# Two heads of a pair in the two partition halves, and their two kinds of score matmul issued in turn

## The chip, the cores and the metric

The kernel runs on one core of a Trainium2 chip. Five engines share the core: TensorE (PE), VectorE (DVE), ScalarE (ACT), GpSimd (POOL) and SyncE (SP), which here only issues DMAs. The metric is the device time of one execution in microseconds. One execution was also taken by the hardware profiler; all times of single instructions come from it.

## The reference

The input x is 16 batches of 256 tokens by 256 features; the context has the same shape. One block of a gated decoder is computed: cross attention with 16 heads of 16 features, then a feed-forward layer whose weights and activations are quantised.

```python
def xattn(Q, K, V):                      # Q = layernorm(x), K = V = ctx
    q = Q @ Wq.T + bq; k = K @ Wk.T + bk; v = V @ Wv.T + bv     # to 16 heads of 16
    attn = softmax(q @ k^T / 4)
    return (attn @ v) @ Wo.T + bo
x = x + tanh(g_xattn[0]) * xattn(layernorm(x), ctx, ctx)
# ffn: x_q = act_qdq(x); up, gate = act_qdq(x_q @ W^T); gate * u16(sigmoid(gate)); act_qdq; @ w_down^T
# act_qdq: 16 bit, one scale for the whole tensor; the weights have 4 bits, one scale for each 32
x = x + tanh(g_ffn[0]) * ffn(layernorm(x))
```

Because each activation scale is a maximum over the whole tensor, the feed-forward part can only begin when the attention of all batches is done.

## The kernel before

`attention` handles 16 batches, each as 8 steps, one for each pair of heads. A step number g runs from -40 to 158; `divmod(g, 8)` gives the batch `it` and the step `j` in it. Every engine runs the same loop over g, and `batch(g, off)` says whether the piece of work with offset off is due; so the order on each engine is written by hand, and semaphores tie the engines together. This is a software pipeline: in step g TensorE computes the scores of batch it+1 and the turned scores of batch it.

Float32 accuracy is had from float16 parts: `qk` holds the high and the low part of q and of k. `stack_q` and `stack_k` (SP, L251 and L261) copy them by DMA into `qst` and `kst`, where the contraction runs over three pieces: high times high, high times low, low times high.

Before the change the two heads of a pair (r = 0, 1) have their rows interleaved in one stack of 96 partitions. `kst` holds both heads; `qst` exists once for each head, with zeros in the rows of the other head, so that one `kst` serves both. Three `memset`s at the start (POOL L769, DVE L647 and L654) write the zeros. Partition 96 holds ones in `kst` and the row maxima in `qst`.

The steps of the attention, with the names that the change and the rows use:

- Scores, L398 (PE): for each of two token tiles tt and each head r, 96 rows x 128 columns of `qst` against 256 columns of `kst`, into `s_ps[tt]`. Four matmuls in a step.
- Row maxima, L670 (DVE): two reductions of 128x512 in a step, one for each `s_ps`. TensorE may write `s_ps[tt]` of the next step when this reduction of the last step is done (`max_done`).
- Turned maxima: TensorE L353 turns the maxima, ACT L518 writes `mrow`, and `load_tops` (SP, L271) copies it into partition 96 of `qst`, in two halves of a batch (TOP0, TOP1), each by two DMAs.
- Turned scores, L414 (PE): for each key tile kt, 97 rows, 512 columns (both heads) into `st_ps[u % 3]`. Two matmuls in a step. ACT L559 takes the exponential of each (`exp_done`).
- Values, L380 (PE): 16 instructions with 32 output columns each, in the steps j = 0, 2, 4, 6.
- Between these, TensorE has one 12-matmul projection (L341) in each odd step: q in j=1, k in j=3, v in j=5, the output in j=7. The turning of xn (L479) is in j=6, the turned maxima in j=0 and j=4.
- DVE has, besides the maxima: y (L680) in j=0, statistics in j=1 and j=3, the low part of q (L641, `ql_done`) in j=2, the low part of k in j=4 with a reciprocal (L706), and one 128x512 operation in each of j=5, 6, 7.

SP issues all DMAs of the attention in one order. From the low part of q on this is: 6 DMAs of `stack_q`, one load of ctx (L242), 3 DMAs of `stack_k` (L265), 2 of TOP0, one of the reciprocals, 4 of `ot`, and the others. The scores of the next batch wait at j = 0 for `stack_loaded`, the turned scores for `top_loaded[0]`; at j = 4 for `top_loaded[1]`.

Of the kernel before, what the change touches and what calls it, by code (L numbers as in the profile page):

```python
# [28 lines left out]
def attention(nc, t, x, ctx, out):  # L29
# [10 lines left out]
    QA = 4  # L40
    ONES = 0x54005400
# [9 lines left out]
    with ExitStack() as es:  # L51
# [42 lines left out]
        kst = sb("kst", [97, 3, PAIRS, S], F16)  # L94
        qst = sb("qst", [97, 3, 2, PAIRS, S], F16)
# [40 lines left out]
        ones_set = sem("ones_set")  # L136
        qst_zeroed = sem("qst_zeroed")
# [94 lines left out]
        def _(sp):  # L232
# [16 lines left out]
            def stack_q(b):  # L249
# [17 lines left out]

            def load_tops(b, hf):
                sp.wait_ge(top_done[hf], b + 1)
                for r in range(2):  # L270
                    sp.dma_start(qst[96:97, b % 3, r, QA * hf:QA * hf + QA, :], mrow[QA * r:QA * r + QA, hf, :]  # L271
                                 ).then_inc(top_loaded[hf], 16)
# [64 lines left out]
        def _(pe):  # L337
# [49 lines left out]
            for g in STEPS:  # L387
                it, j = divmod(g, PAIRS)
                if 0 <= it + 1 < NB:
                    b = it + 1  # L390
                    if j == 0:
                        pe.wait_ge(stack_loaded[b % 2], 144 * (b // 2 + 1))
                    for tt in range(KT):
                        u = UNITS * b + KT * j + tt
                        if u >= 2:
                            pe.wait_ge(max_done, u - 1)
                        for r in range(2):
                            mm = nc.tensor.matmul(s_ps[tt][:, r, :], qst[0:96, b % 3, r, j, tt * P:(tt + 1) * P],  # L398
                                                  kst[0:96, b % 3, j, :], start=True, stop=True)
                        mm.then_inc(s_done, 1)  # L400
                if 0 <= it < NB:
                    b = it
                    if g == 0:
                        pe.wait_ge(ones_set, 1)
                        pe.wait_ge(w_kept, 4)
                    if j == 0:
                        pe.wait_ge(top_loaded[0], 32 * (b + 1))
                    if j == QA:
                        pe.wait_ge(top_loaded[1], 32 * (b + 1))
                    for kt in range(KT):  # L410
                        u = UNITS * b + KT * j + kt
                        if u >= 3:
                            pe.wait_ge(exp_done, u - 2)
                        nc.tensor.matmul(st_ps[u % 3][:], kst[:, b % 3, j, kt * P:(kt + 1) * P],  # L414
                                         qst[:, b % 3, :, j, :], start=True, stop=True).then_inc(st_done, 1)
# [85 lines left out]
        def _(act):  # L501
# [11 lines left out]
            def tops(b, hf):  # L513
                act.wait_ge(top_turned[hf], b + 1)
                if b:
                    act.wait_ge(top_loaded[hf], 32 * b)
# [16 lines left out]
            for g in STEPS:  # L533
# [5 lines left out]
                if (b := batch(g, -14)) is not None:  # L539
                    act.wait_ge(q_done, b + 1)  # L540
                    if b:
                        act.wait_ge(stack_loaded[(b - 1) % 2], 144 * ((b - 1) // 2 + 1))
# [9 lines left out]
                if 0 <= it < NB:  # L552
# [3 lines left out]
                    for kt in range(KT):  # L556
                        u = UNITS * b + KT * j + kt
# [749 lines left out]
```

## Time and profile before

| | us |
|---|---|
| runs of the kernel before | 668.58, 670.52, 671.84 (median 670.52) |
| the profiled execution | 668.55, of which 666.9 from the first to the last instruction |
| TensorE busy | 567.4 |
| VectorE busy | 500.5 |
| ScalarE busy | 436.1 |
| GpSimd busy | 178.9 |
| mean granted TensorE clock | 0.954 |
| row maxima, L670 | 163.4 in 256 instructions |
| exponentials, L559 | 138.9 in 256 |
| scores, L398 | 80.4 in 512 |
| turned scores, L414 | 77.4 in 256 |
| values, L380 | 69.4 in 1024 |

The attention takes up to about 340 us, the rest is the preparation of the feed-forward weights and the feed-forward part. Busy time is the union of an engine's instructions. TensorE's matmuls are pipelined: a row of 0.60 us for 4 matmuls is followed by the next row 0.44 us after its start. For the rate of an engine the distances between starts count, not the lengths.

### The profile page before, as it was taken

Reading aid. Unit: us, or ns where it says so; the run is one execution under the profiler, and the core shown is the slowest. Engines: PE = TensorE matmul, PEld = TensorE weight load, DVE = VectorE, ACT = ScalarE, POOL = GpSimd, SP = SyncE. Lnnn points to the kernel's source line nnn. Section 1 sums busy time; section 2 is a strip of 40 time slices with the busy share of each in tenths; the row PEclk is TensorE's granted clock in tenths of the full one; section 3 lists DMA queues with packets and bytes.
Section 4 is the critical chain, followed back from the end, with each engine's and each line's share of the span. In section 5 each row is a group of like instructions: output and inputs, shape, how many; then the busy total and the mean of one; then the engine's idle time right before and its main releaser. Section 6 shows DMA issues by size and latency. Waiting matters only on the chain. (4 is left out here: it accounts for less than half of the span.)

```text
span 666.9 us, 12176 instructions
## 1 busy us (share of the span) xinstructions
PE 567.4 (85%) x4268; PEld 340.4 (51%) x4268; DVE 500.5 (75%) x772; ACT 436.1 (65%) x609; POOL 178.9 (27%) x193
## 2 busy tenths in 40 slices
PE   0569999999999999999651799999877779949997
PEld 0335666666666666654330344444333334418886
DVE  4498778999999999888864255467999989964441
ACT  2216777778777777876740244549998588859970
POOL 4412235555566565443542000000000000010000
PEclk9979999999999999999885799999999989979999
DMA  6211244544544444552311000000000000011443
GB/s 213 71 47 57 79 121 132 133 136 119 140 111 137 133 124 120 152 150 66 88 55 37 1 0 1 1 0 0 0 0 0 1 0 0 0 63 64 142 141 94
DMA packets 42175, 48.87 MB, mean 73 GB/s; under 512 B 10384, under 2 KB 29456, under 8 KB 42128
## 3 DMA queue, kind: packets, MB, share of 16 engines
q1 hardware_dynamic: 40976, 44.07, 23.1%
q0 software_dynamic: 1152, 4.19, 2.3%
q8 instruction: 27, 0.44, 0.3%
q14 instruction: 20, 0.16, 0.1%
HBM read 24.51 MB, written 8.65 MB: 50 GB/s over the span
## 5 line engine op out<-in xcount | busy, mean ns | idle before, releaser
L670 DVE TENSOR_REDUCE negm<-s_ps 128x2 f32<-128x512 f32 x256 | 163.4, 681 | 32.7 <-PE s_ps L398 32.3
L559 ACT ACTIVATE pt<-st_ps 128x512 f32<-128x512 f32 x256 | 138.9, 596 | 51.7 <-PE st_ps L414 50.7
L937 PE MATMUL pairs<-xq,wut 128*128 x576 | 127.5, 383 | 21.1 <-DVE cmax L1145 12.9
L937 PEld LDWEIGHTS pairs<-xq,wut 128*128 128x128 f16 x576 | 56.7, 99 | 91.9 <-issue 27.7
L398 PE MATMUL s_ps<-kst,qst 96*128 96x256 f16 x512 | 80.4, 275 | 12.8 <-DVE negm L670 7.0
L414 PE MATMUL st_ps<-qst,kst 97*128 97x512 f16 x256 | 77.4, 383 | 3.8 <-ACT pt L559 3.8
L380 PE MATMUL pv_ps<-pt,vt 128*32 128x256 f32 x1024 | 69.4, 389 | 0.7 <-ACT pt L559 0.6
L937 PE MATMUL pairs<-xq,wgt 128*128 (+1 forms) x288 | 64.5, 384 | 0.0
L398 PEld LDWEIGHTS s_ps<-kst,qst 96*128 96x128 f16 x512 | 46.2, 97 | 34.3 <-DVE negm L670 21.1
L1230 POOL PARTITION_ALL_REDUCE vmax<-vmax x4 | 2.3, 582 | 224.2 <-DVE vmax L1118 224.2
L988 PE MATMUL pairs<-wdt,h 128*128 128x256 f16 x384 | 48.4, 277 | 10.0 <-ACT h L1077 10.0
L1134 DVE TENSOR_REDUCE cmax<-gb (+1 forms) x8 | 26.8, 3353 | 36.9 <-ACT gb L1012 36.9
L761 POOL TENSOR_SCALAR xn<-xt,mv,rstd 128x256 f32<-128x256 f32 x30 | 36.5, 1226 | 66.0 <-PE misc L479 65.9
L1012 ACT COPY gb<-pairs 128x1024 f32 (+1 forms) x24 | 24.3, 1012 | 38.5 <-PE pairs L937 38.5
L380 PEld LDWEIGHTS pv_ps<-pt,vt 128*32 128x32 f32 x1024 | 27.0, 110 | 39.0 <-issue 26.3
L988 PEld LDWEIGHTS pairs<-wdt,h 128*128 128x128 f16 x384 | 38.0, 99 | 15.3 <-ACT h L1077 10.5
L937 PEld LDWEIGHTS pairs<-xq,wgt 128*128 128x128 f16 x288 | 28.3, 99 | 33.5 <-issue 1.7
L504 ACT ACTIVATE qk<-misc,bqk_s 128x256 f16<-128x256 f32 x64 | 26.9, 471 | 22.9 <-PE misc L341 22.9
L797 POOL TENSOR_SCALAR lnall<-y,mv,rstd 128x256 f32<-128x256 f32 x28 | 35.1, 1260 | 1.5
L1039 ACT ACTIVATE lnall<-pairs,scal 128x1024 int16<-128x1024 f32 x24 | 25.7, 1109 | 12.0 <-PE pairs L937 7.1
L641 DVE SCALAR_TENSOR_TENSOR qk<-misc,bqk_s,qk 128x256 f16<-128x256 f32 x64 | 27.7, 474 | 5.8 <-ACT qk L504 5.8
L1145 DVE TENSOR_REDUCE cmax<-pairs 128x1024 f32 (+1 forms) x24 | 28.1, 1216 | 5.3 <-PE pairs L937 5.2
(136 smaller groups left out, 991.6 us busy)
## 6 DMA issues: line engine op xcount, KB each, us to landing
qst<-qk SPq DMA_DIRECT2D x96, 64.0 KB, 2.0
kst<-qk SPq DMA_DIRECT2D x48, 128.0 KB, 3.5
xt<-in_x SPq DMA_DIRECT2D x16, 256.0 KB, 4.3
ct<-in_ctx SPq DMA_DIRECT2D x16, 256.0 KB, 3.5
recb<-rec_dram SPq DMA_DIRECT2D x16, 256.0 KB
xr<-in_x SPq DMA_DIRECT2D x16, 256.0 KB, 4.0
out<-y SPq DMA_DIRECT2D x16, 256.0 KB, 4.3
lnall<-out POOLq DMA_DIRECT2D x8, 512.0 KB, 4.2
```

What stands on the lines that cost most here:

```text
L380: mm = nc.tensor.matmul(pv_ps[32 * c:32 * c + 32, u % 2, :], vt[:, b % 3, kt, 8 * (c // 2) + 2 * u + c % 2, :], pt[:, u % 2, c // 2, kt, c ...
L398: mm = nc.tensor.matmul(s_ps[tt][:, r, :], qst[0:96, b % 3, r, j, tt * P:(tt + 1) * P], kst[0:96, b % 3, j, :], start=True, stop=True)
L414: nc.tensor.matmul(st_ps[u % 3][:], kst[:, b % 3, j, kt * P:(kt + 1) * P], qst[:, b % 3, :, j, :], start=True, stop=True).then_inc(st_done, 1)
L504: op = nc.scalar.activation(qk[:, 2 * i, e, :], frm[:, e, :], ACT.Identity, bias=bqk_s[:, i, e:e + 1])
L559: nc.scalar.activation(pt[:, (j // 2) % 2, j % 2, kt], st_ps[u % 3][:], ACT.Exp, scale=1.0 / (WS * WS * HD ** 0.5)).then_inc(exp_done, 1)
L641: op = nc.vector.scalar_tensor_tensor(out=qk[:, 2 * i + 1, e, :], in0=frm[:, e, :], scalar=bqk_s[:, i, e:e + 1], in1=qk[:, 2 * i, e, :], o ...
L670: nc.vector.tensor_reduce(negm[:, b % 2, tt, lo:lo + 5:4], s_ps[tt][:], AX.X, ALU.max, negate=True).then_inc(max_done, 1)
L761: op = nc.gpsimd.tensor_scalar(xn[:, tt, :], xt[:, b % 3, tt, :], mv[:, tt, 0:1], rstd[:, tt:tt + 1], ALU.subtract, ALU.mult)
L797: nc.gpsimd.tensor_scalar(t["lnall"][:, b, tt * D:(tt + 1) * D], y[:, tt, :], mv2[:, tt, 0:1], rstd2[:, tt:tt + 1], ALU.subtract, ALU.mult ...
L937: mm = nc.tensor.matmul(ps[:, p, k, :], w[:, a, dt, f * P:(f + 1) * P], xq[:, b, c, dt, :], start=n == 0, stop=n == len(terms) - 1)
L988: mm = nc.tensor.matmul(ps[:, 2 + d, b, tt * D:(tt + 1) * D], lh, wdt[:, h, f, :], start=n == 0, stop=n == len(terms) - 1)
L1145: nc.vector.tensor_reduce(cmax[:, 1, bass.ds(PR * c + p, 1)], ps[:, p], AX.XY, ALU.max, apply_absolute_value=True).then_inc(u_max, 1)
```

## The change

The rows of a head now lie together: head 0 of a pair in the partitions 0 to 48, head 1 in 64 to 112 (three pieces of 16, then the ones or the maxima). `qst` has no copy for each head and no zeros. Scores and turned scores of one head are 48 or 49 rows in one half of the partitions, each matmul 256 columns wide. They are issued in turn: the scores of head r from its half, the turned scores of head 1-r from the other half. `s_ps[r]` and `st_ps` now hold one head and two tiles. Both waits stand ahead of the group of four, and the waits for `stack_loaded` and `top_loaded` ahead of the step.

```diff
+    HALF = P // 2
+    ROW = (3 * HD, HALF + 3 * HD)
...
-        qst = sb("qst", [97, 3, 2, PAIRS, S], F16)
+        qst = sb("qst", [ROW[1] + 1, 3, PAIRS, S], F16)
...
             def stack_q(b):
-                sp.wait_ge(qst_zeroed, min(b + 1, 3))
                 for r in range(2):
                     for d, i in enumerate((0, 0, 1)):
-                        lo = 32 * d + r
-                        sp.dma_start(qst[lo:lo + 31:2, n, r].rearrange("p j q -> p (j q)"),
+                        lo = HALF * r + HD * d
+                        sp.dma_start(qst[lo:lo + HD, n].rearrange("p j q -> p (j q)"),
...
             def stack_k(b):
-                for d, i in enumerate((2, 3, 2)):
-                    sp.dma_start(kst[32 * d:32 * d + 32, n].rearrange("p j q -> p (j q)"),
-                                 qk[:, i].rearrange("p h q -> p (h q)")).then_inc(stack_loaded[b % 2], 16)
+                for r in range(2):
+                    for d, i in enumerate((2, 3, 2)):
+                        lo = HALF * r + HD * d
+                        sp.dma_start(kst[lo:lo + HD, n].rearrange("p j q -> p (j q)"),
+                                     qk[r:P:2, i].rearrange("p h q -> p (h q)")).then_inc(stack_loaded[b % 2], 16)
             def load_tops(b, hf):
-                for r in range(2):
-                    sp.dma_start(qst[96:97, b % 3, r, QA * hf:QA * hf + QA, :], mrow[QA * r:QA * r + QA, hf, :]
+                sp.dma_start(qst[ROW[0]:ROW[1] + 1:HALF, b % 3, QA * hf:QA * hf + QA, :], mrow[:, hf, :]
...
-                        nc.tensor.matmul(st_ps[u % 3][:], kst[:, b % 3, j, kt * P:(kt + 1) * P],
-                                         qst[:, b % 3, :, j, :], start=True, stop=True).then_inc(st_done, 1)
+                for r in range(2):
+                    us = UNITS * (it + 1) + 2 * j + r
+                    ut = UNITS * it + 2 * j + r
+                    if 0 <= it + 1 < NB and us >= 2:
+                        pe.wait_ge(max_done, us - 1)
+                    if 0 <= it < NB and ut >= 3:
+                        pe.wait_ge(exp_done, ut - 2)
                     for kt in range(KT):
+                        if 0 <= it + 1 < NB:
+                            lo, b = HALF * r, it + 1
+                            scores = nc.tensor.matmul(s_ps[r][:, kt, :], qst[lo:lo + 3 * HD, b % 3, j, kt * P:(kt + 1) * P],
+                                                      kst[lo:lo + 3 * HD, b % 3, j, :], start=True, stop=True)
+                        if 0 <= it < NB:
+                            lo, b = HALF * (1 - r), it
+                            turned = nc.tensor.matmul(st_ps[ut % 3][:, kt, :],
+                                                      kst[lo:lo + 3 * HD + 1, b % 3, j, kt * P:(kt + 1) * P],
+                                                      qst[lo:lo + 3 * HD + 1, b % 3, j, :], start=True, stop=True)
...
-            nc.vector.memset(qst[:, 1].rearrange("p r j q -> p (r j q)").bitcast(I32), 0).then_inc(qst_zeroed, 1)
+            nc.vector.memset(kst[HALF + BLOCK:ROW[1] + 1].rearrange("p n j q -> p (n j q)").bitcast(I32), ONES
...
-            nc.vector.memset(qst[:, 2].rearrange("p r j q -> p (r j q)").bitcast(I32), 0).then_inc(qst_zeroed, 1)
...
-            nc.gpsimd.memset(qst[:, 0].rearrange("p r j q -> p (r j q)").bitcast(I32), 0).then_inc(qst_zeroed, 1)
+            nc.gpsimd.memset(kst[BLOCK:ROW[0] + 1].rearrange("p n j q -> p (n j q)").bitcast(I32), ONES
...
-            nc.gpsimd.memset(kst[96:97].rearrange("p n j q -> p (n j q)").bitcast(I32), ONES).then_inc(ones_set, 1)
```

The columns of the k weights are also permuted on the way in, and the reductions and exponentials read and write one head and two tiles instead of one tile and two heads, with the same shapes.

TensorE, one step with values followed by one with a projection, before (`s_ps` is written by scores, `st_ps` by turned scores, `pv_ps` by values, `misc` by projections):

```order
L398 MATMUL s_ps<-kst,qst 128x256 x4
L414 MATMUL st_ps<-qst,kst 128x512 x2
L380 MATMUL pv_ps<-pt,vt 32x256 x8
L398 MATMUL s_ps<-kst,qst 128x256 x4
L414 MATMUL st_ps<-qst,kst 128x512 x2
L341 MATMUL misc<-ch,wh_k 128x256 x2
```

And in the changed kernel one step, the one with the output projection, and the start of it:

```order
L412 MATMUL s_ps<-kst,qst 128x256
L418 MATMUL st_ps<-qst,kst 128x256
L412 MATMUL s_ps<-kst,qst 128x256
L418 MATMUL st_ps<-qst,kst 128x256
L412 MATMUL s_ps<-kst,qst 128x256
L418 MATMUL st_ps<-qst,kst 128x256
L412 MATMUL s_ps<-kst,qst 128x256
L418 MATMUL st_ps<-qst,kst 128x256
L346 MATMUL misc<-woh,ah 128x256 x2
```

Six matmuls (four of 256 columns, two of 512) became eight of 256 columns, and the two kinds take turns.

SP, from the copies of q of one batch to the reciprocals, before:

```order
L258 DMA qst<-qk 16x4x512 x6
L242 DMA ct<-in_ctx 128x2x256
L265 DMA kst<-qk 32x4x512 x3
L271 DMA qst<-mrow 1x4x256 x2
L312 DMA rec_dram<-rec 128x32
```

And in the changed kernel:

```order
L259 DMA qst<-qk 16x4x512 x6
L244 DMA ct<-in_ctx 128x2x256
L271 DMA kst<-qk 16x4x512 x6
L276 DMA qst<-mrow 2x4x256
L317 DMA rec_dram<-rec 128x32
```

The order is the same; k has six issues of half the size instead of three, and the maxima one instead of two.

## Rows read from the trace of the kernel before

**Rows 1.** The page's 40 equal slices of the span, PE, in tenths busy.

```profile
PE   0569999999999999999651799999877779949997
```

**Rows 2.** Busy time by stretches: start:end, length, each engine's busy us (instructions), granted clock.

```profile
180.00:200.00 20.00, 20.00 (x190) 13.50 (x189) 18.44 (x38) 15.83 (x34) 11.52 (x12) 1.00 0.52 131
...
460.00:530.00 70.00, 53.94 (x246) 23.91 (x245) 69.83 (x67) 60.34 (x25) 1.25 (x1) 1.00 0.00 0
```

**Rows 3.** Timeline of PE, steps 0 and 1 of a batch: start, length, operation.

```profile
230.50 0.60 PE L398 MATMUL s_ps<-kst,qst 96*128 96x256 f16 x4
230.94 0.60 PE L414 MATMUL st_ps<-qst,kst 97*128 97x512 f16 x2
231.47 1.07 PE L380 MATMUL pv_ps<-pt,vt 128*32 128x256 f32 x16
232.47 0.38 PE L353 MATMUL misc<-ident,negm 128*8 128x128 f32 x2
232.69 0.60 PE L398 MATMUL s_ps<-kst,qst 96*128 96x256 f16 x4
...
233.56 0.38 PE L341 MATMUL misc<-xh,wh_q 128*128 128x256 f16 x2
...
234.87 0.60 PE L398 MATMUL s_ps<-kst,qst 96*128 96x256 f16 x4
```

**Rows 4.** Timeline of DVE in the next batch, steps 0 to 5.

```profile
249.98 0.75 DVE L680 SCALAR_TENSOR_TENSOR y<-misc,tgs,xb 128x512 f32<-128x512 f32 x1 [0.22 <-issue]
250.66 1.29 DVE L670 TENSOR_REDUCE negm<-s_ps 128x2 f32<-128x512 f32 x2
...
252.84 1.29 DVE L670 TENSOR_REDUCE negm<-s_ps 128x2 f32<-128x512 f32 x2
254.05 0.87 DVE L641 SCALAR_TENSOR_TENSOR qk<-misc,bqk_s,qk 128x256 f16<-128x256 f32 x2
254.83 1.28 DVE L670 TENSOR_REDUCE negm<-s_ps 128x2 f32<-128x512 f32 x2
...
257.04 1.25 DVE L670 TENSOR_REDUCE negm<-s_ps 128x2 f32<-128x512 f32 x2
...
259.25 1.23 DVE L670 TENSOR_REDUCE negm<-s_ps 128x2 f32<-128x512 f32 x2
```

**Rows 5.** Timeline of SP's DMA issues, from q's stack to the maxima.

```profile
219.85 3.83 SPq L258 DMA_DIRECT2D qst<-qk  x6
223.77 0.53 SPq L242 DMA_DIRECT2D ct<-in_ctx  x1
224.34 1.87 SPq L265 DMA_DIRECT2D kst<-qk  x3
226.25 1.35 SPq L271 DMA_DIRECT2D qst<-mrow  x2
```

**Rows 6.** From issue to landing, the copies into qst, then into kst.

```profile
DMA to landing us min/median/max: 2.0/2.0/4.0
...
DMA to landing us min/median/max: 3.0/3.5/6.5
```

**Rows 7.** Timeline of the start: the three memsets that change.

```profile
9.19 1.79 POOL L769 MEMSET qst<- 97x2048 int32 x1
...
13.83 2.69 POOL L776 MEMSET kst<- 1x3072 int32 x1
14.30 1.76 DVE L654 MEMSET qst<- 97x2048 int32 x1 [0.37 <-issue]
```

**Rows 8.** Timeline of PE, the first scores of the batches 1, 4, 13 and 15.

```profile
56.07 0.90 PE L398 MATMUL s_ps<-kst,qst 96*128 96x256 f16 x4 [0.66 <-DVE negm L670]
...
107.68 0.60 PE L398 MATMUL s_ps<-kst,qst 96*128 96x256 f16 x4
...
265.60 0.60 PE L398 MATMUL s_ps<-kst,qst 96*128 96x256 f16 x4
...
301.82 0.60 PE L398 MATMUL s_ps<-kst,qst 96*128 96x256 f16 x4
```

More of the change, by code:

```diff
@@ L93, in attention @@
         qk = sb("qk", [P, 4, 2, S], F16)
-        kst = sb("kst", [97, 3, PAIRS, S], F16)
-        qst = sb("qst", [97, 3, 2, PAIRS, S], F16)
+        kst = sb("kst", [ROW[1] + 1, 3, PAIRS, S], F16)
+        qst = sb("qst", [ROW[1] + 1, 3, PAIRS, S], F16)
         vt = sb("vt", [P, 3, KT, NH, 32], F32)
@@ L135, in attention @@
         vt_set = sem("vt_set")
-        ones_set = sem("ones_set")
-        qst_zeroed = sem("qst_zeroed")
+        low_ones_set = sem("low_ones_set")
+        high_ones_set = sem("high_ones_set")
         half_set = sem("half_set")
@@ L388, in _ @@
                 it, j = divmod(g, PAIRS)
[L389 to L400, printed above, removed]
@@ new lines, in _ @@
+                if 0 <= it + 1 < NB and j == 0:
+                    pe.wait_ge(stack_loaded[(it + 1) % 2], 192 * ((it + 1) // 2 + 1))
+                if 0 <= it < NB and j == 0:
+                    pe.wait_ge(top_loaded[0], 16 * (it + 1))
+                if 0 <= it < NB and j == QA:
+                    pe.wait_ge(top_loaded[1], 16 * (it + 1))
+                for r in range(2):
[5 more added lines that the diff above has]
+                        pe.wait_ge(exp_done, ut - 2)
+                    for kt in range(KT):
+                        if 0 <= it + 1 < NB:
+                            lo, b = HALF * r, it + 1
+                            scores = nc.tensor.matmul(s_ps[r][:, kt, :], qst[lo:lo + 3 * HD, b % 3, j, kt * P:(kt + 1) * P],
+                                                      kst[lo:lo + 3 * HD, b % 3, j, :], start=True, stop=True)
+                            if kt == KT - 1:
+                                scores.then_inc(s_done, 1)
+                        if 0 <= it < NB:
[3 more added lines that the diff above has]
+                                                      qst[lo:lo + 3 * HD + 1, b % 3, j, :], start=True, stop=True)
+                            if kt == KT - 1:
+                                turned.then_inc(st_done, 1)
@@ L555, in _ @@
                         act.wait_ge(pv_done, 4 * b + j // 2 - 1)
-                    for kt in range(KT):
-                        u = UNITS * b + KT * j + kt
+                    for r in range(2):
+                        u = UNITS * b + 2 * j + r
                         act.wait_ge(st_done, u + 1)
-                        nc.scalar.activation(pt[:, (j // 2) % 2, j % 2, kt], st_ps[u % 3][:], ACT.Exp,
+                        nc.scalar.activation(pt[:, (j // 2) % 2, j % 2, :, 1 - r], st_ps[u % 3][:], ACT.Exp,
                                              scale=1.0 / (WS * WS * HD ** 0.5)).then_inc(exp_done, 1)
@@ L666, in _ @@
                     b = it + 1
-                    for tt in range(KT):
-                        dve.wait_ge(s_done, UNITS * b + KT * j + tt + 1)
-                        lo = 8 * (j // QA) + j % QA
-                        nc.vector.tensor_reduce(negm[:, b % 2, tt, lo:lo + 5:4], s_ps[tt][:], AX.X, ALU.max, negate=True
+                    for r in range(2):
+                        dve.wait_ge(s_done, UNITS * b + 2 * j + r + 1)
+                        at0 = 8 * (j // QA) + QA * r + j % QA
+                        nc.vector.tensor_reduce(negm[:, b % 2, :, at0], s_ps[r][:], AX.X, ALU.max, negate=True
                                                 ).then_inc(max_done, 1)
@@ L1291 @@
         "bq": columns(np.asarray(L0_xattn_bq).reshape(2, 4, 2, HD).transpose(0, 3, 1, 2)),
-        "bk": columns(np.asarray(L0_xattn_bk).reshape(2, 4, 2, HD).transpose(0, 3, 2, 1)),
+        "bk": columns(np.asarray(L0_xattn_bk).reshape(2, 4, 2, HD).transpose(0, 3, 1, 2)),
         "bv": np.asarray(L0_xattn_bv).reshape(2, 2, 2, 2, HD).transpose(0, 3, 1, 4, 2).reshape(P, 2),
```

31 lines of the change are left out of this document (13 added, 18 removed).

## The prediction, made before the changed kernel was run

> **What bounds the kernel now.** I read the page's slices first [rows 1]: TensorE is at nine tenths from about 60 to 300 us, which is the attention, and again in the feed-forward part, which the change leaves alone. The stretches then say who else is near [rows 2]: from 180 to 200 us TensorE is busy for 20.00 of 20 us at full clock, VectorE for 18.44, ScalarE for 15.83. So TensorE sets the pace, and VectorE is 1.6 us in 20 behind it. Most of what TensorE could be relieved of, VectorE does not have to give.
>
> The period of a batch is read from the first scores [rows 8]: nine batches from 107.68 to 265.60 are 17.55 us each. The three before them took (107.68 - 56.07) / 3 = 17.2, the last two before 301.82 took 36.2 together, since a weight load of the feed-forward part comes in between.
>
> TensorE's period comes out of the rows of two steps [rows 3]. Scores: 230.50 to 230.94, 0.44. Turned scores: another 0.44 by their four times 256 columns; the values follow only at 231.47, 0.09 later than that. The values take 1.00 up to the next operation, turned maxima 0.22 (232.47 to 232.69), a projection 1.31 (233.56 to 234.87), and the four instructions that turn xn 0.44 at the same 0.11 each. A batch has 8 x 0.875 + 4 x 1.31 + 4 x 1.09 + 2 x 0.22 + 0.44 = 17.5. That is the measured period, with no room left.
>
> **TensorE after.** The eight new matmuls of a step have 2048 columns, as many as the six old ones. They gain only if a matmul in one half of the rows runs beside one in the other half. The trace of before shows no such pair of row halves. What it shows is that four matmuls of 32 columns each go side by side: the values are 16 instructions of 256 columns in 1.00 us [rows 3], where one after the other, at the 0.11 us that scores of 256 columns take (0.44 for four), they would take 1.75 at least. Bounds for the step's group: 0.44 (full overlap) to 0.875 (none). I take 0.44, nearest to those rows.
>
> The 0.09 before the values stands where the array changes from one arrangement of tiles to another; from turned scores to a projection there is none (232.69 to 233.56 is 0.87, the two groups alone). The halves are a third arrangement. By the order, a step with a projection now has two changes where it had none, the four steps with values have one more where a turned operation follows (j = 0, 4, 6) and none more in j = 2: 4 x 2 + 3 = 11 more in a batch, 11 x 0.09 = 0.99. The Trainium skill (TensorEngine Tiling (Array Packing), Key Properties) says that a change of tiling mode drains TensorE; the gaps of 0.09 agree with it, and by a reading without that rule the 0.99 would fall away.
>
> TensorE after: 17.5 - 8 x 0.435 + 0.99 = 15.0 us a batch, 2.5 less.
>
> **VectorE.** Its rows [rows 4] give two reductions in 1.21 (252.84 to 254.05) and the work between them: y 0.68 (249.98 to 250.66), statistics 252.84 - 250.66 - 1.21 = 0.97, q's low part 0.78, then 257.04 - 254.83 - 1.21 = 1.00, then 259.25 - 257.04 - 1.21 = 1.00, and one operation of about 0.60 in each of steps 5 to 7. Sum: 8 x 1.21 + 0.68 + 0.97 + 0.78 + 1.00 + 1.00 + 1.80 = 15.9. The edit changes the shape of none of them. VectorE needs 15.9 and TensorE 15.0, but they also wait for each other: scores of head r start after the last step's reduction of the same buffer, and a reduction starts 0.42 after its scores did. I walked both engines through the eight steps with these durations and these two waits (and y waiting for GpSimd's xb, as it does before 249.98). For the kernel before this gives 17.57, the measured period; for the kernel after, 16.4. Steps with a projection are longer than VectorE's there, and TensorE can be only one buffer ahead.
>
> **The DMAs of the stacks.** This is what I think is late next. q's low part ends, and SP issues six copies, a load of ctx, three of k and the maxima [rows 5]. The first issue is at 219.85, the batch's scores start at 230.50 [rows 3], 10.65 later. The last k copy is issued at 224.34 + 1.87 - 0.60 = 225.61 and lands 3.5 later at 229.1 [rows 6], 1.4 before it is needed: hidden. After the change SP issues six copies of k at q's pace, 3.83 for six: the last one at 227.6, landing after 2.0, the median of q's copies of the same size, at 229.6. The maxima's single DMA is issued at about 228.2, and the scores now wait for it too, since its wait stands ahead of the step; with the same 2.0 it lands at 230.2. From q's first issue that is 9.8 to 10.4. The same bytes as before share the DMA engines with ctx, so the upper bound is a landing as of the old k copies, 227.6 + 3.5 = 231.1, or 11.2. I take 10.3.
>
> This closes a loop over one batch: scores of step 0, first reduction 0.42 later, VectorE to the end of q's low part (3 x 1.21 + 0.68 + 0.97 + 0.78 = 6.06, and 0.09 to SP), stack, scores. 0.42 + 6.06 + 0.09 + 10.3 = 16.9 us. It is longer than the 16.4 of the two engines, and so it sets the period: 17.55 - 16.9 = 0.65 a batch. SP's own list grows by 3 x 0.64 and shrinks by 2 x 0.68 a batch, about 0.55; it waits for q's low part anyway, so I count nothing for it.
>
> **The rest.** Batches 1 to 3: 17.2 to 16.9 each, 1.0 together; they have no output projection or a late one, and TensorE was less full. Batches 4 to 12: 9 x 0.65 = 5.9. Batches 13 and 14: held by a weight load in the same queue that is not changed; I give them 0.3. The start [rows 7]: GpSimd's memset ahead of the first statistics goes from 1.79 (2048 wide) to the 2.69 of the 3072 wide one, 0.9 later; VectorE's memset of 1.76 between the first xn and its weights goes, and those are waited for by the first q projection. Net 0.8 earlier, less 0.4 for three more issues ahead of the first scores (1.9, less 1.5 of landing): 0.4. After 301.82 there are no projections of q, k, v, VectorE is the fuller engine, and I give 0.3 for the shorter groups and seams. The ones in `kst`, the new strides of exponentials and maxima: the same shapes, on engines with time over; nothing. The end of the attention moves forward by the sum, and the feed-forward part with it.
>
> Sum: 1.0 + 5.9 + 0.3 + 0.4 + 0.3 = 7.9, with the batches as uncertain as the 10.3; I forecast 8.5, since the loop's 10.3 has its likelier bound below. The profiled execution took 668.55, so 660.0; the median of the runs stands 2.0 above it, so 662, and I say 661.
>
> **The rivals.**
>
> *The stacks are in time (A).* If the copies land by 9.8 or less after q's first issue, the two engines set 16.4: 1.15 x 9 + 0.8 x 3 + 1 = 14, so about 655 to 657. For it: q's copies all landed in 2.0 in the median, and smaller copies start earlier. Against it: k's took 3.5 with ctx beside them.
>
> *The stacks eat it all (C).* With 11.2, or with issues that are held up (rows of the same line are as long as landing 4.0 for q, 6.5 for k [rows 6]), the loop is 17.8, TensorE's old period. Then nothing but the start changes: 667 to 670.
>
> *The halves do not overlap (B), the change doesn't do what it says.* Each group stays 0.875 and the 11 changes of arrangement stay too: 18.5 a batch. Place: TensorE's groups of scores; price 0.99 for each of 14 batches from 56.07 to 301.82, less the start: +13, about 683. It decides from the point at which the group takes more than 0.875 - 0.99/8 = 0.75, that is 0.19 us for a pair. Against it: the values' columns do run side by side [rows 3]. The Trainium skill (TensorE: Matmul & The Clock Gate, Packing small matmuls, row/col tiling) gives 3.07 times for four row tiles; an estimate from it for two is 1.5 times, a group of 0.57 and a TensorE period of 16.1. No row here shows it. That is still under the loop's 16.9, so the sum would stay, and B is the less likely for it.
>
> *The clock falls (D).* TensorE will have pauses of half a microsecond in each batch and be busy for 0.85 of the time. Against it: from 460 to 530 us it is busy for 53.94 of 70 us at a granted clock of 1.00 [rows 2]. At the half clock for a tenth of the attention's 270 us, TensorE would do 13.5 us of work too little, of which its new slack of 1.9 in 16.9 takes a ninth: 12 us, about 673. I leave it 3 in 100.
>
> **How the numbers follow.** Forecast (loop of 16.5 to 17.2) 0.52, with 656 to 665 as its own range; A 0.20; C 0.15; B 0.10; D 0.03. The measurement can tell about 0.5% or 3.4 us from no change. Faster takes the forecast but for its edge and A, and a part of C: 0.75. The same is the rest of C and the edge: 0.13. Slower is B, D: 0.12. For 8 in 10 the range reaches over A and C and leaves out B: 653 to 670.
>
> **What would show it.** Scores and turned scores in pairs whose starts lie a few ns apart and a group of 0.44: right; starts 0.11 apart throughout: B. Pauses of about 0.09 on both sides of each group. A period of 16.9 from batch 4 to 12, TensorE waiting at the first scores of a batch for kst or for the maxima's copy, and VectorE idle there; if it waits for VectorE's maxima instead, A. q's first issue to the first scores: 10.3. If the period stays at 17.5 with TensorE busy for less, it is C.

## The result and the profile after

The changed kernel takes 677.77 us (median of 4 runs, 674.49 to 681.07); the kernel before takes 669.55 beside it. The ratio is 1.012, with a 95% interval of 1.006 to 1.018: slower by 1.2%, where I had forecast faster. The profiled execution took 674.49 us with a span of 672.8, against 668.55 and 666.9.

The page's slices of the kernel after, TensorE busy and its granted clock in tenths, answer to [rows 1]:

```profile
PE   0578888998898889996652599999778779949997
PEclk9958899999999999989876699999999989979999
```

The nines of the attention have become eights and nines: TensorE now has time over, and the kernel is no shorter. The stretches that answer to [rows 2], with each engine's busy time, the granted clock, the DMA share and GB/s at the end:

```profile
180.00:200.00 20.00, 17.34 (x209) 9.74 (x210) 17.09 (x36) 14.46 (x31) 12.12 (x13) 1.00 0.43 119
460.00:530.00 70.00, 57.05 (x261) 25.29 (x260) 68.17 (x62) 63.36 (x24) 1.25 (x1) 1.00 0.00 0
```

TensorE is busy for 17.34 of 20 us where it was for 20.00, and VectorE for 17.09 where it was for 18.44. Both wait, so a third party sets the pace. TensorE's timeline at the first scores of a batch names it; it answers to [rows 3]:

```profile
216.00 0.28 PE L412 MATMUL s_ps<-kst,qst 48*128 48x256 f16 x1 [1.29 <-DMA kst<-qk]
216.00 0.28 PE L418 MATMUL st_ps<-qst,kst 49*128 49x256 f16 x1
216.12 0.27 PE L412 MATMUL s_ps<-kst,qst 48*128 48x256 f16 x1
216.12 0.38 PE L418 MATMUL st_ps<-qst,kst 49*128 49x256 f16 x2
216.23 0.27 PE L412 MATMUL s_ps<-kst,qst 48*128 48x256 f16 x1
216.34 0.27 PE L418 MATMUL st_ps<-qst,kst 49*128 49x256 f16 x1
216.34 0.27 PE L412 MATMUL s_ps<-kst,qst 48*128 48x256 f16 x1
216.54 1.07 PE L385 MATMUL pv_ps<-pt,vt 128*32 128x256 f32 x16
217.54 0.38 PE L358 MATMUL misc<-ident,negm 128*8 128x128 f32 x2
```

The halves do overlap. Each pair starts in the same hundredth of a microsecond, the pairs follow at 0.11, and eight matmuls and the change of arrangement take 0.54 (216.00 to 216.54) where they took 0.97 [rows 3]. Ahead of them TensorE was idle for 1.29 us, released by a copy into `kst`. VectorE stood still with it; its row answers to [rows 4]:

```profile
216.43 1.29 DVE L677 TENSOR_REDUCE negm<-s_ps 128x2 f32<-128x512 f32 x2 [1.43 <-PE s_ps L412]
```

SyncE's issues for this batch, which answer to [rows 5]:

```profile
204.93 4.43 SPq L259 DMA_DIRECT2D qst<-qk  x6
209.46 0.53 SPq L244 DMA_DIRECT2D ct<-in_ctx  x1
210.03 3.74 SPq L271 DMA_DIRECT2D kst<-qk  x6
213.82 0.57 SPq L276 DMA_DIRECT2D qst<-mrow  x1
```

The last k copy is issued at 213.2 and the scores start at 216.00. From q's first issue to the first scores it is 11.07 us; it was 10.65. The page's medians from issue to landing, for the two kinds of copy of 64 KB, answer to [rows 6]:

```profile
qst<-qk SPq DMA_DIRECT2D x96, 64.0 KB, 2.5
kst<-qk SPq DMA_DIRECT2D x96, 64.0 KB, 2.5
```

The first scores of batches 1, 4, 13 and 15 answer to [rows 8]:

```profile
55.71 0.28 PE L412 MATMUL s_ps<-kst,qst 48*128 48x256 f16 x1 [0.98 <-ACT wgt L535]
...
111.44 0.27 PE L412 MATMUL s_ps<-kst,qst 48*128 48x256 f16 x1 [1.49 <-DMA kst<-qk]
...
269.46 0.27 PE L412 MATMUL s_ps<-kst,qst 48*128 48x256 f16 x1 [1.26 <-DMA kst<-qk]
...
305.54 0.27 PE L412 MATMUL s_ps<-kst,qst 48*128 48x256 f16 x1 [1.62 <-DMA kst<-qk]
```

From batch 4 to 13 it is 158.02 us, where it was 157.92: a period of 17.56, unchanged. The loss lies at the two ends. From batch 1 to 4 it is 55.73 instead of 51.61, and from batch 15 to the end of the span 367.3 instead of 365.1. In the early stretch the granted clock falls. First the kernel before, from batch 1 to 3, then the kernel after, in the columns of [rows 2]:

```profile
53.00:73.00 20.00, 18.34 (x168) 11.51 (x166) 15.29 (x29) 15.95 (x31) 5.51 (x6) 1.00 0.28 76
73.00:90.00 17.00, 16.64 (x158) 10.20 (x157) 13.28 (x27) 13.36 (x29) 4.59 (x6) 1.00 0.28 80
```

```profile
55.00:75.00 20.00, 15.11 (x158) 8.05 (x160) 14.64 (x28) 13.94 (x28) 5.58 (x6) 0.91 0.23 66
75.00:94.00 19.00, 15.83 (x176) 8.31 (x178) 13.29 (x26) 13.37 (x27) 4.49 (x5) 0.91 0.26 72
```

The granted clock of 0.91 is a mean of stretches at 1.00 (2.4 GHz) and some at 0.50 (1.2 GHz). One fall follows on the longest pause: the first scores of batch 2 at 74.98 came after 2.93 us of idleness. The next longest, 2.62 us ahead of the scores at 93.83, brought none.

### The profile page after: what moved, and what is told of

The parts are those of the page before. It is cut to its first block and busy times, and to the rows that moved or that the text cites. A ratio compares the mean times of both kernels' runs of the same rounds, so it can differ in the third digit from the quotient of the medians.

```text
span 672.8 us, 12907 instructions
## 1 busy us (share of the span) xinstructions
PE 542.8 (81%) x4524; PEld 304.8 (45%) x4524; DVE 498.5 (74%) x771; ACT 434.7 (65%) x609; POOL 176.7 (26%) x192
## 5 line engine op out<-in xcount | busy, mean ns | idle before, releaser
L566 ACT ACTIVATE pt<-st_ps 128x512 f32<-128x512 f32 x256 | 139.3, 597 | 51.8 <-PE st_ps L418 50.5
L412 PE MATMUL s_ps<-kst,qst 48*128 48x256 f16 x512 | 85.3, 280 | 39.6 <-DMA kst<-qk 19.0
L418 PE MATMUL st_ps<-qst,kst 49*128 49x256 f16 x512 | 82.0, 277 | 4.5 <-ACT pt L566 4.5
L412 PEld LDWEIGHTS s_ps<-kst,qst 48*128 48x128 f16 x512 | 35.8, 96 | 82.2 <-DVE negm L677 36.4
L385 PE MATMUL pv_ps<-pt,vt 128*32 128x256 f32 x1024 | 71.0, 396 | 1.2 <-ACT pt L566 1.1
L418 PEld LDWEIGHTS st_ps<-qst,kst 49*128 49x128 f16 x512 | 35.3, 95 | 9.0 <-ACT pt L566 5.9
L797 POOL TENSOR_TENSOR at<-ot,recb 128x512 f32<-128x512 f32 x16 | 20.3, 1269 | 56.6 <-DMA recb<-rec_dram 56.6
```

The costliest lines, as they stand in the source:

```text
L385: mm = nc.tensor.matmul(pv_ps[32 * c:32 * c + 32, u % 2, :], vt[:, b % 3, kt, 8 * (c // 2) + 2 * u + c % 2, :], pt[:, u % 2, c // 2, kt, c ...
L412: scores = nc.tensor.matmul(s_ps[r][:, kt, :], qst[lo:lo + 3 * HD, b % 3, j, kt * P:(kt + 1) * P], kst[lo:lo + 3 * HD, b % 3, j, :], start ...
L418: turned = nc.tensor.matmul(st_ps[ut % 3][:, kt, :], kst[lo:lo + 3 * HD + 1, b % 3, j, kt * P:(kt + 1) * P], qst[lo:lo + 3 * HD + 1, b % 3 ...
L566: nc.scalar.activation(pt[:, (j // 2) % 2, j % 2, :, 1 - r], st_ps[u % 3][:], ACT.Exp, scale=1.0 / (WS * WS * HD ** 0.5)).then_inc(exp_don ...
```

## The experiments

The theory was: a list of issues on SyncE, longer by three k copies, sets the period through the time from q's first issue to the first scores, and eats what the halves give. The first rival: TensorE's new arrangement itself costs the time (no overlap, a lower clock). The second: ScalarE, VectorE and TensorE together have no more to give. All figures of a batch below are means over batches 4 to 13 of each profiled execution, in us; "list" is q's first issue to SyncE's last k issue, "first scores" is q's first issue to the first scores, "to q" is first scores to the next batch's first q issue. The period is (first scores of batch 13 - first scores of batch 4) / 9. It is first scores + to q but for up to 0.24, since batch 4 counts in the one and not in the other. The medians come from several sessions, in which the kernel before took 669.55 to 671.29; each ratio is to the runs of the kernel before in the same session.

| kernel | list | first scores | to q | period | median us | ratio to before (95%) |
|---|---|---|---|---|---|---|
| before | 6.33 | 10.66 | 6.92 | 17.55 | 669.55 | |
| after | 8.40 | 11.08 | 6.48 | 17.56 | 677.77 | 1.012 (1.006 to 1.018) |
| e1, ctx later | 8.44 | 11.29 | 6.64 | 18.05 | 674.96 | 1.006 (1.003 to 1.010) |
| e2, 3 by ScalarE | 6.30 | 11.03 | 6.84 | 17.98 | 665.26 | 0.994 (0.992 to 0.997) |
| e3, before with 6 | 8.26 | 11.12 | 7.05 | 18.17 | 681.36 | 1.018 (1.015 to 1.022) |
| e4, same half | 8.42 | 11.05 | 6.98 | 17.79 | 681.59 | 1.015 (1.008 to 1.022) |
| e5, pauses filled | 8.34 | 11.14 | 6.73 | 17.81 | 673.85 | 1.004 (1.001 to 1.006) |
| e6, 3 by GpSimd | 6.28 | 9.84 | 6.88 | 16.58 | 665.70 | 0.994 (0.992 to 0.996) |
| e7, ScalarE, later | 6.60 | 10.10 | 6.63 | 16.76 | 657.31 | 0.980 (0.976 to 0.984) |
| e8, short list | 6.17 | 9.72 | 6.85 | 16.63 | 658.60 | 0.983 (0.980 to 0.987) |
| e9, e7 and filled | 6.20 | 9.92 | 6.73 | 16.72 | 660.96 | 0.986 (0.983 to 0.989) |
| e10, before, short | 4.79 | 10.66 | 6.92 | 17.55 | 668.61 | 0.997 (0.996 to 0.999) |
| e11, e4 and short | 6.14 | 9.74 | 6.88 | 16.65 | 661.03 | 0.983 (0.980 to 0.986) |
| e12, e7 and e1 | 5.85 | 9.82 | 6.78 | 16.64 | 656.34 | 0.979 (0.976 to 0.983) |
| e13, one half | 6.41 | 11.47 | 7.35 | 18.83 | 686.46 | 1.025 (1.023 to 1.027) |

**e3_before_split: the longer list alone, in the kernel before.**

```diff
-for d, i in enumerate((2, 3, 2)):
-    sp.dma_start(kst[32*d:32*d+32, n], qk[:, i]).then_inc(...)          # 128 KB
+for r in range(2):
+    for d, i in enumerate((2, 3, 2)):
+        sp.dma_start(kst[32*d+16*r:32*d+16*r+16, n], qk[64*r:64*r+64, i]).then_inc(...)   # 64 KB
```

> The kernel before with each copy of k cut in two (six of 64 KB for three of 128 KB); TensorE's order untouched. Theory 1: q's first issue to landing grows from about 9.8 to 10.5 to 11; with 6.9 from first scores to q's issue the period is 17.5 to 17.9 and TensorE waits for kst in some batches: median 670 to 675. If the six copies are not what costs: 669.5 as before.

It costs more than expected, 11 us, with TensorE's work as it was. SyncE's rows of one batch, to be set beside [rows 5]:

```profile
208.09 4.82 SPq L258 DMA_DIRECT2D qst<-qk  x6
213.01 0.53 SPq L242 DMA_DIRECT2D ct<-in_ctx  x1
213.59 3.74 SPq L267 DMA_DIRECT2D kst<-qk  x6
```

Six issues of 64 KB take 3.74, three of 128 KB took 1.87: an issue costs 0.62 for either size. The first scores come 11.12 after q's first issue, and the period is no longer TensorE's but 7.05 + 11.12 = 18.17. The changed kernel has the same list (11.08), but the shorter groups bring q forward (6.48 instead of 6.92), and the two cancel.

**e8_short_list: the list shortened, nothing else.** It leaves out the third pieces of q and k from batch 3 on, as its expectation says; e10, e11 and e13 have the same cut.

```diff
-for d, i in enumerate((0, 0, 1)):
+for d, i in enumerate((0, 0, 1)[:3 if b < 3 else 2]):
 ...
-for d, i in enumerate((2, 3, 2)):
+for d, i in enumerate((2, 3, 2)[:3 if b < 3 else 2]):
```

> The changed kernel, which from the fourth batch on leaves out the four copies of the third pieces (two of q, two of k): those rows keep the values of an earlier batch. SyncE's list loses 4 issues of 0.64 us, 2.5 us. Theory: the list decides the period at 17.56 us; with 8.5 us from q's first issue to the last landing it would allow 15.0, so TensorE, VectorE and ScalarE decide, and if their floor is the 16.4 us that I predicted, the period falls to it, 11 batches times 1.1 us: 660 to 664 us. Rival: their floor is 17.3 us, as the issues on ScalarE suggest, then 670 to 674 us. If the list has no part in it, 677 us.

658.60 us, somewhat better than the theory's 660 to 664; the period is 16.62 or 16.63 in each batch from 7 to 13. SyncE's rows, then the stretch:

```profile
197.15 2.53 SPq L263 DMA_DIRECT2D qst<-qk  x4
199.78 0.53 SPq L248 DMA_DIRECT2D ct<-in_ctx  x1
201.32 2.46 SPq L275 DMA_DIRECT2D kst<-qk  x4
203.82 0.58 SPq L280 DMA_DIRECT2D qst<-mrow  x1
```

```profile
180.00:200.00 20.00, 19.07 (x226) 10.70 (x222) 19.10 (x43) 16.11 (x35) 14.34 (x18) 1.00 0.41 127
```

The k copies begin 4.17 after q's and no sooner, though the issue of ctx is over at 3.2: they wait for k's low part on VectorE, which ends at 201.29. TensorE (19.07) and VectorE (19.10 of 20) are now equally full. I take this as the floor of the engines, which I had walked to 16.4: e6, e11 and e12 come to 16.58 to 16.65 as well.

**e10_before_short: the same cut in the kernel before.**

> The kernel before, which from the fourth batch on leaves out its three copies of the third pieces (two of q, one of k); the rows keep an earlier batch's values. Theory: before, TensorE's own 17.5 us a batch decide and the stacks are in time, so a list shorter by 1.9 us changes nothing: period 17.55 us, 668 to 671 us, ratio 0.998 to 1.002. Rival: the stacks decide before as they do after; then the period falls to 16.6 to 16.9 us and the time to 659 to 662 us, and all of what the short list gave the changed kernel says nothing of the halves.

The period stays at 17.55 and the first scores at 10.66. The runs are 0.3% shorter (0.996 to 0.999, just under the expected 0.998 to 1.002), the profiled one is not (668.54 against 668.55). So the kernel before waited for TensorE, not for the stacks, and the 1.7% of e8 need the changed matmuls.

**e2_act_issues and e7_act_after_take: three of the six k copies issued by ScalarE.** The full computation again. In e2 they stand ahead of the copy of the finished values (`take`), in e7 behind it, as here:

```diff
 # SyncE, stack_k: only the three copies of the even heads
 # ScalarE, step j = 5:
 if (b := batch(g, 5)) is not None:
     take(b, 0)
+if (b := batch(g, -11)) is not None:
+    act.wait_ge(kl_done, b + 1)
+    for d, i in enumerate((2, 3, 2)):
+        act.dma_start(kst[HALF+HD*d:HALF+HD*d+HD, b % 3], qk[1:P:2, i]).then_inc(...)
```

> The changed kernel with head 1's three copies of k issued by ScalarE's queue, in the step where SP issues head 0's. Theory 1: the list on SP is 1.9 us shorter, q's first issue to first scores falls from 11.0 to about 9.1, under the 9.8 where TensorE and VectorE take over; period 16.4 to 16.6, median 662 to 667. Theory 2: unchanged, 676 to 679. If ScalarE's own time becomes short (12.9 us of work a batch before, 1.9 of issue more), exponentials are late and the period is 17 or more with TensorE waiting for exponentials.

The time was as expected, but not the period: 17.3 in most batches (two in which the granted clock fell took 20.2 and 20.4), although the stacks had landed at 9.7. ScalarE's timeline shows what held it:

```profile
226.59 1.05 ACT L565 ACTIVATE pt<-st_ps 128x512 f32<-128x512 f32 x2
227.20 1.88 ACTq L574 DMA_DIRECT2D kst<-qk  x3
229.18 0.58 ACT L517 COPY ot<-pv_ps 128x512 f32<-128x512 f32 x1 [1.54 <-issue]
```

The copy out of `pv_ps` waits 1.54 behind three issues, and TensorE's next values wait for the copy (8.4 us in 150). That led to e7:

> As the run with three k copies issued by ScalarE, but placed behind the copy of the finished values in the same step instead of ahead of it. Theory: that copy stood idle for about 1.6 us a batch behind the issues, and TensorE's values waited for it (10.3 us in 185 us of the trace); with the copy first, the period falls from 17.3 by 0.3 to 0.6 us, and the time to 657 to 662 us. Rival: something else held that step, and moving the issues by 0.6 us changes nothing: 663 to 667 us. If the three copies now land last, the first scores come up to 0.6 us later and the gain is lost: also 665.

```profile
217.16 0.59 ACT L565 ACTIVATE pt<-st_ps 128x512 f32<-128x512 f32 x1
217.63 0.59 ACT L517 COPY ot<-pv_ps 128x512 f32<-128x512 f32 x1
217.71 1.27 ACTq L576 DMA_DIRECT2D kst<-qk  x2
219.09 1.09 ACT L565 ACTIVATE pt<-st_ps 128x512 f32<-128x512 f32 x2 [0.86 <-PE st_ps L417]
```

The issues now run beside the copy, and what idles behind them waits for TensorE anyway. 657.31 us: 2% faster than the kernel before and 20 us faster than the changed one, by who issues three of the copies, and where. Of the 16.5 us between the two profiled executions the nine periods of 16.76 instead of 17.56 give 7. Most of the rest lies in the batches around them (from batch 1 to 4 it is 50.5 instead of 55.7, from 13 to 15 34.0 instead of 36.1), where this execution also has fewer falls of the clock.

**e6_pool_issues: the three copies issued by GpSimd.**

```diff
+if (b := batch(g, -12)) is not None:      # GpSimd, ahead of normalise
+    pool.wait_ge(kl_done, b + 1)
+    ... pool.dma_start(...) x3, with a semaphore of their own
```

> The changed kernel, with the three k copies of the second head of each pair issued by GpSimd in the step in which k's low parts are done, instead of by SyncE behind the other three. Theory: the list of issues on SyncE decides, and ScalarE's own work must not be cut into: SyncE's list is that of the kernel before again (9.7 us from q's first issue to the last stack landed), GpSimd has idle time of more than half the period, so with ScalarE undisturbed the period falls to the 16.4 to 16.9 us of the engines and the time to 655 to 661 us. Rival 1: the two engines' floor is the 17.3 us that the issues on ScalarE showed, whoever issues, then 663 to 667 us. Rival 2: GpSimd issues slowly (over 1.2 us a copy) or starts late behind its own work, its three copies land after the others, the chain stays at 11 us, and the time at 672 to 680 us.

The period is the shortest of all, 16.58, as the theory said, and GpSimd issues a copy in 0.55. The time, 665.70, is that of rival 1. Its profiled execution loses in the first batches: batch 4 starts at 109.7, where it is 105.5 in e7. 1.3 us of that stand at the first scores of batch 1 already. The rest lies in the periods 1 to 2 and 3 to 4, 18.75 and 17.99 against 17.02 and 16.49, and in both the granted clock falls: it is 0.57 from 57 to 65 us and 0.66 from 91 to 96.

**e1_late_ctx: the ctx load moved behind the stacks and the maxima on SyncE.**

```diff
-if (b := batch(g, -28)) is not None and b >= 2: load_c(b)      # between q and k
 ... stack_k(b) ... load_tops(b, 0)
+if (b := batch(g, -27)) is not None and b >= 2: load_c(b)
```

> The changed kernel with SP's load of ctx moved from between the copies of q and k to behind the maxima's copy; nothing else. Theory 1 (the list of stack copies sets the period: 6.5 us from the first scores of a batch to q's first issue, 11.0 from there to the next batch's first scores): the 11.0 shortens by 0.3 to 1.0, the period of the batches 4 to 12 falls from 17.56 to 16.6 to 17.2, and the median time from 677.8 to 667 to 673. Theory 2 (TensorE or VectorE or their waits for each other set it): no change, 17.5 and 676 to 679. Theory 3 (the lower TensorE clock in the first 90 us is the loss): period 17.5, no change.

A miss. The list did not get shorter (8.44), since k's copies still wait for k's low part, at least 4.16 after q's first issue (5.16 in the mean), and single issues still take 1.2 to 1.7 us. The interval reaches into that of the changed kernel.

**e5_fill_pause: does the pause cost clock?**

```diff
+if g in (0, 8, 16):
+    pe.wait_ge(max_done, UNITS * (it + 1))
+    for _ in range(5): ...       # four score matmuls on the last batch's stacks, overwritten later
```

> The changed kernel, with 20 more score matmuls (on the stacks of the batch before, their results overwritten) issued at three seams, those ahead of the first scores of batches 1, 2 and 3, while TensorE waits there for the stacks. Theory: the granted clock falls to 0.5 at 75.7 us because of the pause of 2.93 us just before it, and the loss of the first two periods (19.26 and 18.86 us against 16.9 before) is in part that of the clock. Then no granted clock of 0.5 at 75 to 79 us, first scores of batch 3 at 92.0 to 93.3 us instead of 93.8, total 1 to 2 us less than 674.5 (672 to 675, ratio to the kernel before 1.005 to 1.010). Rival: the clock has nothing to do with the pause, then the fall stays, and the total is 674 to 679. In both, the periods stay above 17.5 us, since the list of stack copies decides them.

Stretches of e5, then of the kernel after:

```profile
75.00:79.00 4.00, 4.00 (x54) 2.36 (x52) 2.81 (x5) 3.93 (x9) 1.16 (x1) 1.00 0.03 5
91.00:95.00 4.00, 3.98 (x35) 1.54 (x36) 1.69 (x3) 2.33 (x5) 1.16 (x1) 0.57 0.26 66
```

```profile
75.00:79.00 4.00, 4.00 (x36) 1.61 (x37) 1.89 (x3) 2.53 (x6) 1.15 (x1) 0.59 0.18 62
91.00:95.00 4.00, 1.38 (x24) 0.77 (x24) 2.64 (x5) 1.94 (x5) 2.28 (x2) 1.00 0.22 54
```

The fall at 75 to 79 is gone and batch 3 begins at 91.02 instead of 93.83; another fall comes at 91 to 95, behind a seam that was filled too. The median is 3.9 us lower, but the intervals of the two ratios meet at 1.006. So the pause may have had a part in the fall at 75; that pauses at seams decide where the clock falls is not shown. How much a fall costs, e8 shows better. Up to the stacks of batch 2 it is the same program as the kernel after, and its first scores are at 56.26 and 73.58 for batches 1 and 2: a period of 17.32 at a granted clock of 1.00, where the kernel after took 19.27 at 0.91 and the kernel before 16.85. Of the 2.4 us lost there about 0.5 is the change with its longer list; 1.9 go with a fall that one execution of the same instructions has and another has not.

**e9_take_fill and e12_take_late: e7 with the edit of e5 (at two seams) or of e1.**

> The kernel with head 1's k copies issued by ScalarE behind the copy of the finished values (657.3 us), with the 20 extra matmuls of the pause experiment at two seams, ahead of batches 2 and 3. Theory: its granted clock of 0.5 at 73 to 77 us goes, the next two periods are 1 to 2 us shorter together, 655 to 657 us. Rival: the fall only moves to a later pause (as it did to 91 to 95 us when this was tried with the list on SyncE), and the time is 657 to 660 us.

> The kernel with head 1's k copies issued by ScalarE behind the copy of the finished values, with the context's load moved behind the stacks and the maxima on SyncE. Theory: its stacks still come late in some batches (first scores 10.1 us after q's first issue where 9.7 is the engines' own), and a list shorter by one issue of 0.6 us takes 0.1 us a batch off: 655.5 to 657 us. Rival: no change, 657 to 658 us, or the context comes late and it is 658 to 662 us.

e9 has a granted clock of 1.00 from 72 to 78 us, where e7 has 0.72, but then 0.88 from 275 to 300, where e7 has 1.00, and is 3.7 us slower, though the intervals of the two ratios meet: the rival, and worse. But e12, with nothing filled, has 0.92 from 275 to 300 as well, so this later fall can't be put down to the filling. e12 comes to 656.34, and its runs (653.15 to 660.79) lie on both sides of all of e7's (656.01 to 657.93); the two can't be told apart. Both beat the kernel before by 2%.

**e4_same_half, e11_same_short and e13_one_half: what is the overlap worth?**

```diff
-lo, b = HALF * (1 - r), it        # turned scores: the other head's half
+lo, b = HALF * r, it              # e4, e11: the half of the scores beside it
+lo, b = 0, it                     # e13, and lo = 0 in the scores too: head 0 in place of head 1
```

> The changed kernel with the turned scores taken from the same half as the scores beside them, so that four matmuls in a row are in one half and only the seam between the heads can overlap. If the overlap of the halves is worth what the trace shows (group 0.44 instead of 0.875), the group is 0.77 to 0.875, TensorE needs 17.7 to 18.5 a batch and is the bound again: median 680 to 690. If TensorE's time no longer matters at all, 677.8.

> The changed kernel with both matmuls of a pair on the same row half (no overlap) and, from the fourth batch on, without the four copies of the third pieces. Theory: with the list out of the way what is left is TensorE without overlap, which the sum puts at 17.5 to 18.5 us a batch, against 16.63 with overlap: 674 to 682 us, so the overlap is worth 0.9 us or more a batch, some 16 us in all (658.6 with it). Rival: the overlap was never needed, VectorE and ScalarE decide: then the period is 16.6 to 16.9 us and the time 658 to 663 us.

e4 is 3.8 us above the changed kernel, at the low end of what was expected, and the intervals of the two overlap. e11 shows that its premise was wrong: with the short list and "no overlap" the period is 16.65, that of e8. Its rows:

```profile
225.03 0.29 PE L416 MATMUL s_ps<-kst,qst 48*128 48x256 f16 x2
225.15 0.28 PE L422 MATMUL st_ps<-qst,kst 49*128 49x256 f16 x2
225.27 0.28 PE L416 MATMUL s_ps<-kst,qst 48*128 48x256 f16 x2
225.38 0.28 PE L422 MATMUL st_ps<-qst,kst 49*128 49x256 f16 x2
```

Each row holds two matmuls whose starts lie 13 ns apart: the second head's four ran beside the first head's four, though they stand behind them in the program. (Of each head's two scores only the second counts up `s_done`, and the two that do not start at 225.034 and 225.047.) The overlap had not been taken away, and both runs say nothing against it. e13 takes it away, with the short list. It computes head 0 in place of head 1 too, by the same number of instructions:

> The kernel with the short list of stack copies (658.6 us), in which all score matmuls and turned score matmuls read the lower row half: head 0 is computed in place of head 1 too, with the same instructions in the same order. In the run with both matmuls of a pair on one half, the rows still show starts 13 ns apart, since the second head's four ran beside the first head's four; so no run has yet taken the overlap away. Here nothing can overlap. Theory: a group of eight takes 8 x 0.11 = 0.88 us and not 0.55, TensorE needs 16.63 + 8 x 0.33 = 19.3 us a batch if it had no slack, and 15.0 + 8 x 0.44 = 18.5 by the sum of the prediction, less up to 1.0 for changes of arrangement: 17.5 to 18.5 us a batch, 670 to 684 us. Rival: VectorE and ScalarE hold the period at 16.63 us, the overlap is worth nothing, 657 to 663 us.

```profile
226.21 0.28 PE L416 MATMUL s_ps<-kst,qst 48*128 48x256 f16 x1
226.33 0.27 PE L422 MATMUL st_ps<-qst,kst 49*128 49x256 f16 x1
226.44 0.27 PE L416 MATMUL s_ps<-kst,qst 48*128 48x256 f16 x1
...
227.00 0.27 PE L422 MATMUL st_ps<-qst,kst 49*128 49x256 f16 x1
227.20 0.39 PE L350 MATMUL misc<-xh,wh_q 128*128 128x256 f16 x2
```

```profile
180.00:200.00 20.00, 20.00 (x196) 13.00 (x194) 17.46 (x36) 14.93 (x31) 10.31 (x11) 1.00 0.39 108
```

Starts are 0.11 apart, a group takes 0.99, TensorE is busy for 20.00 of 20, and the period is 18.83 with the same short list. The overlap is worth 18.83 - 16.63 = 2.2 us a batch; without it even the short list leaves the kernel 16 us slower than before.

## Why the prediction was wrong

The step that failed is the 10.3 us of "The DMAs of the stacks", measured at 11.08, and with it the choice of the loop's 16.9 over rival C.

- **The list.** I let q's issues take 3.83 as in one batch and started k's at 4.49; they start at 5.10 in the mean: in eight of the ten batches one issue of the list takes 1.2 to 1.8 us. Such issues stand in the trace of before too. The batch that I read was a good one: its last k copy landed 9.26 after q's first issue, where the mean over batches 4 to 13 is 9.75 and batch 7 has 10.47, 0.2 short of the first scores. I had seen the long landings in [rows 6] and given them to C. For the landing I took 2.0, the median of q's old copies; the new ones take 2.5. So 7.75 + 2.0 + 0.5 for the maxima became 8.40 + 2.56 + 0.12: 11.08. The maxima's copy, which I thought would be last, is about level with the stacks: the first scores start 0.05 to 0.16 after the last k landing. The other half of the loop was right: 6.57 predicted, 6.48 measured. 6.48 + 11.08 = 17.56; that this is TensorE's old period of 17.55 is an accident.
- **Batches 4 to 12:** -5.9 predicted, +0.1 measured. **The start:** -0.4, and it is 55.71 - 56.07 = -0.4. That may be luck: e8 and e11, which start by the same program, have 56.26 and 56.29.
- **Batches 1 to 3:** -1.0 predicted, +4.1 measured. There the list is against 9.73 in the kernel before and not 10.66, so a chain of 11.28 and 10.98 loses from its first tenth on, and first scores to q rose from 7.12 and 7.19 to 7.98 and 7.88 at a granted clock of 0.91. I had taken one price of the list for all batches. But e8 puts only 0.5 of the first period's 2.4 us on the list (above), and in e5 the second period, at a clock of 1.00, takes 17.78 where the kernel after took 18.86 and the one before 16.92. The rest, some 3 of the 4 us, goes with the clock. e12, with a list of 5.85 and a clock of 1.00, starts batch 3 at 87.26.
- **Batches 13 and 14:** -0.3, and -0.1. **After 301.82:** -0.3 predicted, +2.2 measured. Up to the last values it is only 0.1 of that (36.47 us from the first scores of batch 15, where it was 36.34); the 2.1 come behind them, where the change has no part in the instructions. The change isn't shown to cost this: e10, the program of the kernel before in this stretch, takes 366.5 where that one took 365.1, and over all kernels here it is 363.5 to 369.8. I gave the clock 0.03; rival D priced it through a busy share of 0.85, where its own 15.0 in 16.9 gives 0.89 and 0.87 was measured. The sum is +5.9 for the profiled execution; the other runs of the changed kernel have lower mean clocks (0.917 to 0.929 against its 0.939) and are up to 6.6 us longer. So the list explains why batches 4 to 12 gained nothing. That the kernel came out slower than before lies in the first periods, where most of the loss goes with falls of the clock, and in the end, whose 2.2 us stay open.
- **TensorE.** Right: starts together, group 0.54 with its change of arrangement, which costs 0.09 to 0.10 on the side of a projection too. From e13, TensorE's own sum with overlap is 18.83 - 8 x (0.99 - 0.55) = 15.3; I had 15.0.
- **The rivals.** A's engines need 16.63, not 16.4; where the stacks are in time (e7, e12) the time is 657.3 and 656.3, against the 655 to 657 it gave. B's 18.5 is 18.83 in e13. C's mechanism is what happened in batches 4 to 12, priced at 667 to 670; it lacked the first batches and the clock.

The Trainium skill (DMA: Bandwidth & Descriptors, Rules for kernel authors) advises one transfer of 128 partitions over two of disjoint halves, and says (in the section Issuing engines are not separate DMA queues) that issuing from several engines saves only the sequencer's time, which is usually small beside the transfer. The runs agree with the advice (e3: +11 us) and show that the sequencer's time can be had back (e7: -20 us); but it is here 0.62 us for each of 13 issues in a row, and decides.

## What to carry to other kernels

Before an edit multiplies the number of DMAs on one queue, write out the chain from the first issue to the last landing for every phase of the kernel, with the mean and not the best issue time; a gain on the busiest engine counts only down to that chain. If the chain is too long, issue part of it from another engine, and place those issues behind whatever that engine owes to others. An experiment meant to remove an overlap has to show in its rows that the overlap is gone.

## What the runs showed of the hardware

- Matmuls in different row halves overlap without being issued in turn. In e11 the fifth instruction of a group (225.047) starts before the second (225.154), and the group takes 0.56 as against 0.54 in turn. The Trainium skill (TensorE: Matmul & The Clock Gate, Part 3: Packing small matmuls — row/col tiling, The mechanism) says that matmuls start strictly in program order; here they don't, and the measurement decides.
- Two row halves of 256 columns give 0.99 against 0.55 for the group with its change of arrangement, 0.88 against 0.44 without it: twice, not the 1.5 times that the prediction estimated from the figure of the Trainium skill (TensorE: Matmul & The Clock Gate, Packing small matmuls, row/col tiling) for four row tiles.
- An issue of a DMA costs 0.62 us on SyncE for 64 KB and 128 KB alike, about the same on ScalarE, and 0.55 on GpSimd. From 100 to 285 us, 9 to 14 of SyncE's issues took over 0.9 us in each of the kernels before, after and e1 to e4, up to 2.0; why stays open.
- From 56 to 300 us the kernel before, its TensorE busy for 241 of 244 us, shows a granted clock of 1.00 throughout; the kernel after falls to 0.50 at 58.7, 75.7 and 287.4, the last two just behind pauses of 2.93 and 2.06 us. Eleven pauses of 1.05 to 2.62 us between 93 and 270 us brought no fall. Where a pause was filled (e5, e9) the fall there was gone, and others came later; what decides them stays open.
